# A selective scan whose driving term lies in PSUM and whose 1/A lies in the summing matrices

## What is computed

```python
delta = jax.nn.softplus(x @ W_delta.T + delta_bias)
B_sel = (x @ W_B.T).reshape(B, Lx, Dx, Nx)
C_sel = (x @ W_C.T).reshape(B, Lx, Dx, Nx)
dA = delta[..., None] * A
A_bar = jnp.exp(dA)
B_bar = (A_bar - 1.0) / dA * delta[..., None] * B_sel
Bx = B_bar * x[..., None]

def step(h, inp):
    a_t, bx_t, c_t = inp
    h = a_t * h + bx_t
    y_t = jnp.sum(h * c_t, axis=-1)
    return (h, y_t)
```

## Time and profile before

| | us |
|---|---|
| median of 3 runs | 1066.62 |
| lowest and highest | 1063.59, 1070.86 |
| profiled execution | 1061.23 |
| its span in the profile | 1059.4 |

### The profile page before, as it was taken

How to read it: one execution, slowest core, us unless ns; L and a number is a source line. 1 busy time by engine, 2 the same in 40 slices (tenths; PEclk the granted TensorE clock), 3 DMA queues, 4 the chain that set the end, 5 groups by cost and what they waited for, 6 DMA issues and landing times. The chain is left out here.

```text
span 1059.4 us, 19253 instructions
## 1 busy us (share of the span) xinstructions
PE 907.0 (86%) x6375; PEld 736.4 (70%) x6375; DVE 437.9 (41%) x1187; ACT 305.4 (29%) x620; POOL 328.0 (31%) x331
## 2 busy tenths in 40 slices
PE   6888999798788987999889999999788967798882
PEld 3665888565467646777567899999665854698871
DVE  1234222222135137999565222222152874545442
ACT  2222122314334315444231122222233122043430
POOL 0002455000102115888112444444201000256670
PEclk9977899898688999999999999999899687599996
DMA  9215599300000022120023699898800600488894
GB/s 372 86 42 179 192 309 293 90 1 1 0 2 2 1 101 90 60 64 27 1 92 139 213 304 317 290 318 303 249 15 21 204 2 26 143 260 269 274 270 96
DMA packets 56627, 151.43 MB, mean 143 GB/s; under 512 B 8035, under 2 KB 18422, under 8 KB 56310
## 3 DMA queue, kind: packets, MB, share of 16 engines
q1 hardware_dynamic: 47094, 126.72, 35.7%
q0 software_dynamic: 9472, 23.93, 8.3%
HBM read 137.11 MB, written 13.51 MB: 142 GB/s over the span
## 5 line engine op out<-in xcount | busy, mean ns | idle before, releaser
L1237 POOL DMA_INDIRECT L_xr<-x_rows_L,L_rows_in x96 | 97.2, 1013 | 41.9 <-issue 37.0
L1862 DVE TENSOR_TENSOR L_act<-L_hid,bank 116x512 f32<-116x512 f32 (+1 forms) x56 | 35.8, 640 | 160.5 <-ACT L_hid L1831 108.6
L1751 POOL DMA_INDIRECT y_rows_L<-L_yb,L_rows_out x56 | 55.4, 989 | 106.9 <-ACT L_yb L1837 95.1
L1831 ACT ACTIVATE L_hid<-bank 116x512 f32<-116x512 f32 (+1 forms) x56 | 31.3, 559 | 158.8 <-PE bank L1801 141.1
L1795 PE MATMUL bank<-L_xtb,L_w 128*116 128x128 f32 (+1 forms) x464 | 59.2, 282 | 0.0
L1136 POOL TENSOR_TENSOR ssm_w_low<-ssm_wbc,ssm_w_high 128x512 fp32r<-128x512 f32 x24 | 49.0, 2041 | 31.8 <-ACT ssm_w_high L1101 31.8
L1557 POOL COPY L_xrow<-L_xrow 96x384 f32<-96x384 f32 x3 | 1.5, 497 | 182.7 <-ACT L_xrow L1541 182.7
L1795 PEld LDWEIGHTS bank<-L_xtb,L_w 128*116 128x116 f32 (+1 forms) x464 | 56.5, 191 | 0.2
L1183 DVE TENSOR_TENSOR_SCAN ssm_state<-ssm_decay,ssm_drive 128x576 f32<-128x576 f32 x24 | 55.5, 2311 | 0.8
L230 PE MATMUL bank<-par_const 128*128 128x512 f32 x72 | 50.2, 829 | 0.2 <-issue 0.2
L1811 PE MATMUL bank<-L_w,L_act 116*128 116x192 f32 (+1 forms) x232 | 46.0, 339 | 3.7 <-ACT L_yb L1837 2.1
(11 more groups left out here) (444 smaller groups left out, 2021.8 us busy)
## 6 DMA issues: line engine op xcount, KB each, us to landing
L_w<-in_L2w SPq DMA_DIRECT2D x20, 696.0 KB
L_more<-in_L2w SPq DMA_DIRECT2D x20, 696.0 KB
L_w<-in_L2w SPq DMA_DIRECT2D x20, 384.0 KB
L_more<-in_L2w SPq DMA_DIRECT2D x20, 384.0 KB
L_w<-in_L0w SPq DMA_DIRECT2D x12, 576.0 KB
L_more<-in_L0w SPq DMA_DIRECT2D x12, 576.0 KB
ssm_wbc<-in_wBC SPq DMA_DIRECT2D x24, 256.0 KB
L_w<-in_L3w SPq DMA_DIRECT2D x16, 384.0 KB
```

Source lines behind the costliest of these rows:

```text
L1237: pool.indirect_dma_start(self.xr[j][:, :], None, self.x_rows[:, :], bass.IndirectOffsetOnAxis(ap=at, axis=0))\
L1751: pool.indirect_dma_start(X.y_rows[:, :], bass.IndirectOffsetOnAxis(ap=rows_out[h][:, j:j + 1], axis=0), y[s + j][:, :], None).then_inc(st ...
L1831: act.activation(hid[j][:, :, :], cols(gate_bank[j % 2][0:N, 0:C * R], C), ACT.Silu).then_inc(acted, 1)
L1862: dve.tensor_tensor(act_out[j][:, :, :], hid[j][:, :, :], cols(up_bank[j % 2][0:N, 0:C * R], C), ALU.mult)\
```

## The change

1. `drive` no longer has SBUF buffers. It is the PSUM pair 3 (banks 6 and 7, 576 columns on end), which the rest sums used. VectorE makes it as a product of a new SBUF tile `grown` and B read straight from PSUM; the scan reads it there.
2. ScalarE no longer reads B. It makes `less` = decay - 1 from decay, with a wait for its own decay, and GpSimd makes `grown` = less * x.
3. 1/A moves to the summing matrices: for each tile ScalarE scales the identity or `restsum` by 1/A, partition by partition, into `sum_w`, and `sum_states` uses it as weights. The sum waits for it (`weighed`).
4. The eight rest tiles come first (`REST_TILES`), the 16 wide ones after. Both sum into banks 4 and 5. The rest sums are copied to `y_rest` by ScalarE in its loop step 9, before the first wide sum.
5. TensorE's order: B(0) and C(0) ahead of the loop; then in step t B(t+1), sum(t-1), C(t+1). B(t+1) waits for `driven` (VectorE has read B(t)), C(t+1) for `read_out` (it has read C(t)).

```diff
-    WIDE_AT, REST_AT = 2, 3
+    SUM_AT, DRIVE_AT = 2, 3
...
-        decay, bsel, bx, drive, state, out = ([sb(f"{x}{i}", [128, TOKENS]) for i in range(NB)]
-                                              for x in ("decay", "bsel", "bx", "drive", "state", "out"))
+        decay, less, grown, state, out = ([sb(f"{x}{i}", [128, TOKENS]) for i in range(NB)]
+                                          for x in ("decay", "less", "grown", "state", "out"))
+        sum_w = [sb(f"sum_w{i}", [128, 128]) for i in range(NB)]
+        drive = T.psum[:, 1024 * DRIVE_AT:1024 * DRIVE_AT + TOKENS]
...
         def of(t):
 
-            return int(t % 3 == 2)
+            return int(t < REST_TILES)
...
             def sum_states(t):
                 pe.wait_ge(read_out, t + 1)
-                rest = of(t)
-                first, last = (t == 2, t == n_tiles - 1) if rest else (t == 0, t == n_tiles - 2)
+                pe.wait_ge(weighed, t + 1)
+                if t == REST_TILES:
+                    pe.wait_ge(rest_out, 1)
+                n = 64 if of(t) else 128
                 for s in range(2):
...
+                    mm = pe.matmul(T.bank[2 * SUM_AT + s][0:n, 0:HALF], sum_w[t % NB][:, 0:n],
+                                   out[t % NB][:, HALF * s:HALF * s + HALF], start=t in (0, REST_TILES),
+                                   stop=t in (REST_TILES - 1, n_tiles - 1))
                 mm.then_inc(summed, 1)
...
             project(0, 0, b_made)
+            project(0, 1, c_made)
+            pe.wait_ge(relu_made, 2)
             for t in range(n_tiles):
                 if t + 1 < n_tiles:
                     pe.wait_ge(low, t + 2)
-                    pe.wait_ge(b_out, t + 1)
+                    pe.wait_ge(driven, t + 1)
                     project(t + 1, 0, b_made)
                 if t:
-                    pe.wait_ge(read_out, t)
-                project(t, 1, c_made)
-                if t == 1:
-                    pe.wait_ge(relu_made, 2)
-                if t:
                     sum_states(t - 1)
+                if t + 1 < n_tiles:
+                    pe.wait_ge(read_out, t + 1)
+                    project(t + 1, 1, c_made)
             sum_states(n_tiles - 1)
...
             for t in range(n_tiles):
-                if t >= NB:
-                    act.wait_ge(bx_made, t - NB + 1)
-                act.wait_ge(b_made, t + 1)
-                act.activation(cols(bsel[t % NB][:, :], 2), T.pair(0)[:, :, 0:HALF], ACT.Copy, scale=inv_a[:, t:t + 1])\
-                    .then_inc(b_out, 1)
                 if t == 0:
                     act.wait_ge(delta_made, 1)
                 if t >= NB:
                     act.wait_ge(scanned, t - NB + 1)
                 act.activation(decay[t % NB][:, :], delta[:, of(t), :], ACT.Exp, scale=p["sA"][:, t:t + 1]).then_inc(decayed, 1)
+                act.wait_ge(decayed, t + 1)
+                if t >= NB:
+                    act.wait_ge(grown_made, t - NB + 1)
+                act.activation(less[t % NB][:, :], decay[t % NB][:, :], ACT.Copy, bias=-1.0).then_inc(lowered, 1)
+                if t == 0:
+                    act.wait_ge(inverted, 1)
+                if t >= NB:
+                    act.wait_ge(summed, t - NB + 1)
+                n = 64 if of(t) else 128
+                act.activation(sum_w[t % NB][:, 0:n], p["restsum"] if of(t) else p["ident"], ACT.Copy, scale=inv_a[:, t:t + 1])\
+                    .then_inc(weighed, 1)
                 if t + 3 < n_tiles:
                     split_high(t + 3)
-            act.wait_ge(summed, n_tiles)
-            act.copy(cols(y_rest[:, :], 2), T.pair(REST_AT)[0:64, :, 0:HALF]).then_inc(y_out, 1)
+                if t == REST_TILES + 1:
+                    act.wait_ge(summed, REST_TILES)
+                    act.copy(cols(y_rest[:, :], 2), T.pair(SUM_AT)[0:64, :, 0:HALF]).then_inc(rest_out, 1)
...
-                pool.wait_ge(b_out, t + 1)
                 if t == 0:
                     pool.wait_ge(xs_in, 2)
-                pool.tensor_tensor(bx[t % NB][:, :], bsel[t % NB][:, :], xs[:, of(t), :], ALU.mult).then_inc(bx_made, 1)
+                pool.wait_ge(lowered, t + 1)
+                pool.tensor_tensor(grown[t % NB][:, :], less[t % NB][:, :], xs[:, of(t), :], ALU.mult).then_inc(grown_made, 1)
...
-                dve.wait_ge(decayed, t + 1)
-                dve.wait_ge(bx_made, t + 1)
-                dve.scalar_tensor_tensor(drive[t % NB][:, :], d[:, :], 1.0, bx[t % NB][:, :], ALU.subtract, ALU.mult)\
-                    .then_inc(driven, 1)
+                dve.wait_ge(grown_made, t + 1)
+                dve.wait_ge(b_made, t + 1)
+                dve.tensor_tensor(cols(drive, 2), cols(grown[t % NB][:, :], 2), T.pair(0)[:, :, 0:HALF], ALU.mult).then_inc(driven, 1)
...
-                dve.tensor_tensor_scan(st[:, :], d[:, :], drive[t % NB][:, :], 0.0, ALU.mult, ALU.add).then_inc(scanned, 1)
+                dve.tensor_tensor_scan(st[:, :], d[:, :], drive, 0.0, ALU.mult, ALU.add).then_inc(scanned, 1)
```

More of the change, by code:

```diff
@@ L34 @@
 SCAN_TILES = 24
+REST_TILES = 8
 WARM = 6
@@ L1009, in selective_scan @@
         x_high, x_low, x_mixed, x_top = (sb(x, [128, TOKENS], F32R) for x in ("x_high", "x_low", "x_mixed", "x_top"))
-        decay, bsel, bx, drive, state, out = ([sb(f"{x}{i}", [128, TOKENS]) for i in range(NB)]
-                                              for x in ("decay", "bsel", "bx", "drive", "state", "out"))
+        decay, less, grown, state, out = ([sb(f"{x}{i}", [128, TOKENS]) for i in range(NB)]
+                                          for x in ("decay", "less", "grown", "state", "out"))
+        sum_w = [sb(f"sum_w{i}", [128, 128]) for i in range(NB)]
+        drive = T.psum[:, 1024 * DRIVE_AT:1024 * DRIVE_AT + TOKENS]
         y_wide, y_rest = sb("y_wide", [128, TOKENS]), sb("y_rest", [64, TOKENS])
         loaded = [sem(f"loaded{i}") for i in range(NW)]
[L1014 to L1018, removed]
+        (laid, pre_made, abs_made, relu_made, soft, delta_made, xs_in, x_split, inverted, high, low, b_made, c_made, decayed,
+         lowered, grown_made, weighed, driven, reset, scanned, read_out, summed, rest_out, y_out, y_laid) = map(
+            sem, ("laid", "pre_made", "abs_made", "relu_made", "soft", "delta_made", "xs_in", "x_split", "inverted", "high",
+                  "low", "b_made", "c_made", "decayed", "lowered", "grown_made", "weighed", "driven", "reset", "scanned", "read_out",
+                  "summed", "rest_out", "y_out", "y_laid"))
         wd = cols(T.full["sD"], 2)
@@ L1153, in _ @@
             dve.tensor_copy(x_top[64:128, :], T.zero[64:128, 0:TOKENS]).then_inc(x_split, 1)
-            dve.reciprocal(inv_a[:, :], p["sA"])
+            dve.reciprocal(inv_a[:, :], p["sA"]).then_inc(inverted, 1)
             for j in range(2):
@@ L1190, in _ @@
             dve.wait_ge(summed, n_tiles)
-            dve.tensor_copy(cols(y_wide[:, :], 2), T.pair(WIDE_AT)[:, :, 0:HALF]).then_inc(y_out, 1)
+            dve.tensor_copy(cols(y_wide[:, :], 2), T.pair(SUM_AT)[:, :, 0:HALF]).then_inc(y_out, 1)
             for s in range(2):
@@ L2260, in scan_channels @@
     for t in range(SCAN_TILES):
-        pair, r = t // 3, t % 3
-        d[t] = lane if r < 2 else 128 + lane % 64
-        n[t] = 2 * pair + (r if r < 2 else lane // 64)
+        d[t] = 128 + lane % 64 if t < REST_TILES else lane
+        n[t] = 2 * t + lane // 64 if t < REST_TILES else t - REST_TILES
     return d, n
```

2 lines of the change are left out of this document (1 added, 1 removed).

## The result

| | before | after |
|---|---|---|
| median of 8 runs each, us | 1065.17 | 1054.38 |
| lowest and highest, us | 1060.94, 1076.92 | 1048.59, 1060.19 |
| profiled execution (span), us | 1061.2 (1059.4) | 1052.8 (1051.0) |

The ratio is 0.989, with a 95% interval of 0.986 to 0.9919. The prediction was 1054.5 us, within 1049 to 1063. It put the line between faster and unchanged at about 1% (10.7 us) and gave both sides nearly the same chance; the measured gain lies on that line: 10.8 us between the medians, 1.1% in the ratio, with 0.8 to 1.4% in the interval.

A forecast was written before the change was run, and what follows sets the result against it. VectorE's four-instruction loop, 4.23 us a tile, was taken as the bound. Start, 22 TensorE periods (82.3 us), a 0.3 hitch and the end put the y_wide copy at 504.7 for 516.84: 1066.6 - 12.1 = 1054.5 us, range 1049 to 1063.

The forecast's parts named there:

- the scan: VectorE's loop: with drive in PSUM the scan goes from a 2.31 us median to 1.36, a tile to 3.01.
- TensorE is late next: Once VectorE is freed, TensorE's floor sets the pace: 3.62 us a wide tile, 3.95 a rest tile.
- bubbles at changes of group: Rival, chance 0.16: each change of group on TensorE costs 0.05 to 0.11 us, giving back 3.3 to 7.3.
- the start: First tiles: B(1) starts at 415.75 us after TensorE's stop, runs at half clock, and C(1) ends at 419.85.
- the hitch: ScalarE's loop 9 waits for sum 7 before copying y_rest, so drive(10) misses B(11)'s start; 0.3 us lost.
- the scan still waits: Rival, chance 0.11: the scan keeps 2.31 us, VectorE sets the pace at 3.96, 5 us given back, 1059.5.

The follow-up runs named there:

- e4: The changed kernel with two of five product terms left out of each projection, six matmuls for ten; stage 89.24 us, against 105.19 for the change.
- e7: The changed kernel with rest sums made onto 128 weight columns, 64 of them zero; stage 102.47 us, ratio to before 0.9889.
- e1: The changed kernel with drive back in SBUF buffers, all else kept; stage 105.58 us, against 105.19 for the change, ratio to before 0.9915.
- e5: The kernel before with drive in PSUM, rest tiles first and both sums in one pair of banks; stage 103.54 us, ratio to before 0.995.
- e2: The changed kernel with TensorE's old order, C(0) behind B(1) again; stage 125.99 us, ratio to before 1.0151.
- e3: The kernel before with TensorE's new order alone; stage 129.97 us, against 115.99 before, ratio 1.0151.

## Why the prediction held, and where it didn't

**Right: the scan.** VectorE's tile was taken as 3.01 with scan 1.36 and drive 0.75. The trace has 1.354 and 0.76, and e4, with TensorE out of the way, shows scans 3.00 or 3.01 apart in 21 of 23 steps. Writing PSUM costs VectorE nothing visible.

**Right: TensorE is late next.** Its floor of 3.62 and 3.95 was measured at 3.63 and 3.96; the only idle time that the profile shows for it between 407 and 500 us is that before B(1). No bubbles at changes of group:

```profile
442.10 0.29 PE L1057 MATMUL bank<-ssm_x_top,ssm_w_low 128*128 128x288 f32 x1
442.33 1.18 PE L1068 MATMUL bank<-ssm_out,ssm_sum_w 128*64 128x288 f32 x4
443.44 0.40 PE L1057 MATMUL bank<-ssm_x_high,ssm_w_high 128*128 128x288 f32 x1
443.68 0.30 PE L1057 MATMUL bank<-ssm_x_low,ssm_w_high 128*128 128x288 f32 x1
```

The steps of 0.23 and 0.24 around this rest sum are the 0.1 on each side that the earlier trace rows already held in its 1.31, and e7 removes them; they belong to the 64 columns (and the 64 output partitions that go with them), not to the wait.

**Mis-sized: the start.** It was given 3.2 us of half clock from B(1) on, as the earlier trace rows show it behind a stop of 2.48 us, though the prediction's own stop was longer (410.2 to 415.75). The stop was 3.95 us, and half clock lasted 5.6:

```profile
407.66 0.29 PE L1057 MATMUL bank<-ssm_x_top,ssm_w_low 128*128 128x288 f32 x1
411.89 0.58 PE L1057 MATMUL bank<-ssm_x_high,ssm_w_high 128*128 128x288 f32 x1 [3.95 <-DVE bank L1186]
412.27 0.44 PE L1057 MATMUL bank<-ssm_x_low,ssm_w_high 128*128 128x288 f32 x1
...
417.31 0.39 PE L1057 MATMUL bank<-ssm_x_high,ssm_w_low 128*128 128x288 f32 x1
417.54 0.30 PE L1057 MATMUL bank<-ssm_x_mixed,ssm_w_high 128*128 128x288 f32 x1
```

23 matmuls were slow instead of 13: ten more at 0.24 - 0.13 = 0.11 make 1.1 us, and the step of 0.38 behind the first another 0.14. B(1) itself began 15.06 us after the first `xs` copy, for a predicted 14.90. With 0.2 for periods of 3.63 and 3.96 and the hitch taken off again, that is 1.1 + 0.14 + 0.16 + 0.2 - 0.3 = 1.3, the difference between the 12.1 us predicted and the 10.8 measured.

**Wrong: the hitch.** The copy to `y_rest` did hold ScalarE by 1.77 us, and drive(10) waited 1.29 us for GpSimd; TensorE lost nothing, so the 0.3 was zero.

**Wrong: the price of the rival "the scan still waits".** I gave it 5 us, from 3.96 in every tile. e1 is that case, and it costs 0.4. The step that failed is that the scan keeps its median length whatever the rest does, so that VectorE's 3.96 rules the wide tiles too, where TensorE needs 3.62. In the rest tiles the scan did take 2.32 and the loop 3.96, but TensorE needs 3.96 there too. In the wide tiles the scan got in first, took 1.50, and GpSimd paid: its two instructions need 2.7 us alone and 3.69 with the wait, for TensorE's 3.63. That these two lie so close is luck; the prediction has no term for GpSimd's wait.

**Not in the prediction: which part earns it.** The text credited the drive in PSUM, and e5 shows that it suffices, with 12.5 us, the new order of tiles included. But the text took the rest of the change to be free. The new order and the shorter path of B have to come together (e2, e3), and beside the drive in PSUM they cost 1.65 us of stage at the start. Conversely e1, which has those two and not the drive in PSUM, comes within 0.4 us of the change. There are two roads to about the same pace, and their gains don't add: 12.5 and 10.4 alone, 10.8 together.

**The absolute time** came within 0.1 us of 1054.5, and luck is in that: it was subtracted from a median 1.4 us above that of the eight runs, while the stage gave 1.3 us less.

The sentence ahead of the first piece of TensorE's order says that C takes its weights from buffer 2 and B from buffer 0; the rows printed there have it the other way round. Nothing was worked out from it.
